# A depthwise causal convolution moved from TensorE (diagonal matmuls) to VectorE (multiply-adds with a per-partition scalar)

## The reference

```
mixed = einsum('btd,cd->btc', x, W_qkv)                  # 3072 channels
c = conv_general_dilated(mixed^T, conv_w, padding=[(K - 1, 0)],
                         feature_group_count=CONV_DIM)   # K = 4 taps, one filter per channel
mixed = silu(c); q, k, v = split(mixed)                  # 16 heads of 64
beta = sigmoid(x W_b); g = -exp(A_log) * softplus(x W_a + dt_bias)
S = S * exp(g_t) + k_t (v_t b_t)^T;   o_t = q_t S        # scan over time
out = out * rsqrt(mean(out^2) + 1e-6) * silu(z)
x = x + out W_out
W = einsum('abcd,cefg->abefdg', G1, G2)                  # FFN weights, real and imaginary
x = x + complex_linear(layernorm(x), W_real, W_imag)
```

## Time and profile before

| what | us |
|---|---|
| runs of the kernel before | 2817.29 and 2794.29, median 2805.79 |
| profiled execution, its own time | 2800.42 |
| its span on the slowest core (core 4) | 2798.9 |
| spans of the eight cores | 2769.6 to 2798.9 |

### The profile page before, as it was taken

The page is one execution under the profiler, slowest core; times in us unless marked ns, Lnnn a source line. Parts: engine busy times, 40 slices in busy tenths (PEclk is TensorE's granted clock), DMA queues, the critical chain, the costliest instruction groups (busy, mean ns, idle before and its releaser), DMA issues.

```text
span 2798.9 us, 17445 instructions; the slowest of 8 cores (2769.6 to 2798.9 us)
## 1 busy us (share of the span) xinstructions
PE 1217.3 (43%) x5440; PEld 478.7 (17%) x5440; DVE 707.4 (25%) x1023; ACT 342.2 (12%) x570; POOL 124.6 (4%) x217
## 2 busy tenths in 40 slices
PE   0005427246254276244447434437624444743444
PEld 0002112021121131021122011213101112201121
DVE  1143141240331410222330222232022223022322
ACT  0001102002011011011102111111201110211111
POOL 1230000000000000100000000000010000000000
PEclk9999557556575585556567556668556666755666
DMA  8654210201101201200011110010220001011001
GB/s 127 144 168 84 40 19 17 26 19 42 1 20 42 19 4 45 6 19 20 19 42 23 27 5 19 19 42 19 49 6 19 19 19 42 20 29 6 19 19 27
DMA packets 149624, 94.79 MB, mean 34 GB/s; under 512 B 133291, under 2 KB 134064, under 8 KB 149536
## 3 DMA queue, kind: packets, MB, share of 16 engines
q0 software_dynamic: 43360, 36.00, 10.8%
q1 hardware_dynamic: 106176, 57.69, 7.3%
HBM read 99.76 MB, written 11.67 MB: 40 GB/s over the span
## 4 chain that ended last, share of the span: by engine, by line
PE 42%; DVE 19%; DMA 15%; ACT 10%; issue 8%; DVEq 2%; POOL 2%; ACTq 1%; POOLq 0%; SPq 0%
PE ps L281 35%; DMA s_gamb<-scr 4%; ACT s_mixed L281 4%; PE psS L281 4%; PE psT L281 3%; DVE s_dsb L281 3%; DMA s_eaq<-scr 3%; DVE s_bn L281 3%; DMA s_dsb<-convdiag 3%; DVE s_Sall L281 2%; ACT L281 2%; DVEq L280 2%; ACT s_dsb L281 2%; DVE s_x2a L281 1%; DVE s_gatedc L281 1%
## 5 line engine op out<-in xcount | busy, mean ns | idle before, releaser
L281 PE MATMUL ps<-s_mixed,s_dwin 128*128 128x512 bf16 x640 | 296.9, 617 | 178.1 <-ACT s_mixed L281 143.6
L281 PE MATMUL ps<-s_lnxT,s_wqkvT 128*128 128x512 bf16 (+1 forms) x1344 | 299.7, 387 | 9.2 <-DVE s_lnxT L281 7.9
L281 PE MATMUL psT<-s_i128b,s_lnx 128*128 128x128 bf16 x256 | 32.4, 307 | 393.7 <-DVE s_lnx L281 393.7
L281 PEld LDWEIGHTS ps<-s_lnxT,s_wqkvT 128*128 128x128 bf16 x1344 | 132.8, 101 | 174.5 <-issue 35.8
L281 PE MATMUL psT<-s_i128b,s_mixed 128*128 128x128 bf16 x512 | 58.8, 286 | 206.4 <-DMA s_a<-s_dsb 84.6
L281 PE MATMUL psT<-s_i128b,s_gatedc 128*128 128x128 bf16 x256 | 32.4, 307 | 248.7 <-DVE s_Sbf L281 161.2
L281 PEld LDWEIGHTS ps<-s_mixed,s_dwin 128*128 128x128 bf16 x640 | 69.0, 126 | 402.5 <-issue 402.0
L281 ACT ACTIVATE s_mixed<-ps 128x512 bf16<-128x512 f32 x160 | 95.8, 599 | 326.9 <-PE ps L281 326.9
L281 DVE COPY s_mixed<-s_halo 128x72 bf16<-128x72 bf16 x8 | 1.8, 227 | 464.8 <-ACT s_mixed L281 464.8
L281 DVE CAST s_mixed<-ps 128x512 bf16<-128x512 f32 (+1 forms) x88 | 57.9, 658 | 238.5 <-PE ps L281 238.5
L281 PE MATMUL ps<-s_wbig,s_gatedT 128*128 128x512 bf16 x256 | 96.9, 562 | 15.8 <-DVE s_gatedT L281 15.8
(11 more groups left out here) (119 smaller groups left out, 1174.7 us busy)
## 6 DMA issues: line engine op xcount, KB each, us to landing
s_dwin<-diagbf SPq DMA_DIRECT2D x160, 128.0 KB, 2.2
s_xa<-xpre SPq DMA_DIRECT2D x16, 512.0 KB, 4.3
s_xa<-xown SPq DMA_DIRECT2D x16, 512.0 KB, 3.9
s_xr<-xown SPq DMA_DIRECT2D x16, 512.0 KB, 4.0
s_wqkvT<-wqkvT POOLq DMA_DIRECT2D x1, 6144.0 KB, 41.9
s_eaq<-scr POOLq DMA_DIRECT2D x32, 128.0 KB, 5.4
y<-s_x2a SPq DMA_DIRECT2D x8, 512.0 KB, 2.9
y<-s_x2b SPq DMA_DIRECT2D x8, 512.0 KB, 2.9
```

What stands on the lines that cost most here:

```text
L281: r = a(*args, **kw)
```

## The change

The diagonal matrices go, with their six rounds of load and store, the scratch, the 160 loads of `dwin`, and the 640 matmuls. In their place the host packs the taps into `convw`, 128 x 96 f32 (one column for each chunk and tap), which SP loads once. VectorE computes each chunk in f32 in one of two halves of `z_chunk` (512 columns each, free at this point): one tensor_scalar for the first tap, then three scalar_tensor_tensor (multiply by the tap, add the sum so far). ScalarE's Silu reads that half and writes the chunk in `mixed`, as before. From the third chunk on VectorE waits for the Silu of two chunks earlier. The wait of VectorE for the six stores before the first tile goes; a wait for SP's small loads comes in behind the memsets.

```
-    d_diagbf = nc.dram_tensor("diagbf", [24, 4, 128, 128], BF16, kind="Internal").ap()
...
+    sL.inc(SY.dma_start(out=convw_sb[:], in_=d_convw), 16)
...
     sV.inc(V_.memset(ones16f[:], 1.0))
-    for grp in range(6):
-        p0 = grp * 16
-        if grp > 0:
-            s_dgm.wait(G_)
-        s_dg.inc(G_.dma_start(
-            out=dsb_t[:].rearrange("p (f c) -> p f c", f=16),
-            in_=diag_flat[p0:p0 + 16].rearrange("f p c -> p f c")), 16)
-        s_dg.wait(SY)
-        s_dgm.inc(SY.dma_start(
-            out=diagbf_flat[p0:p0 + 16].rearrange("f p c -> p f c"),
-            in_=dsb_t[:].rearrange("p (f c) -> p f c", f=16)), 16)
+    sL.wait(V_)
...
-    s_dgm.wait(V_)
...
+        accs = [z_chunk[:, 0:512], z_chunk[:, 512:1024]]
+        sS.wait(V_)
+        conv_vf = {}
+        conv_sf = {}
         for i_cc, cc in enumerate(cc_list):
-            dhalf = i_cc % 2
+            acc = accs[i_cc % 2]
+            base = cc * 515
             if i_cc >= 2:
-                w = evac_cnt.get(("conv", i_cc - 2))
-                SY.wait_ge(w[0].h, w[1])
-            s_dw[dhalf].inc(SY.dma_start(
-                out=dwin[:, dhalf * 512:(dhalf + 1) * 512].rearrange("p (f c) -> p f c", f=4),
-                in_=diagbf_flat[cc * 4:(cc + 1) * 4].rearrange("f p c -> p f c")), 16)
-            s_dw[dhalf].wait(T)
-            sV.wait(T)
-            sS.wait(T)
-            ph = ps2[:, dhalf * 512:(dhalf + 1) * 512]
-            for tapn in range(4):
-                sT.inc(T.matmul(ph, dwin[:, dhalf * 512 + tapn * 128: dhalf * 512 + (tapn + 1) * 128],
-                                mixed[:, cc * 515 + tapn: cc * 515 + tapn + 512],
-                                start=(tapn == 0), stop=(tapn == 3)))
-            evac_cnt[("conv", i_cc)] = (sT, sT.fence())
-            sT.wait(S_)
-            sS.inc(S_.activation(out=mixed[:, cc * 515 + 3: cc * 515 + 515], in_=ph,
+                sS.wait(V_, conv_sf[i_cc - 2])
+            V_.tensor_scalar(out=acc, in0=mixed[:, base: base + 512],
+                             scalar1=convw_sb[:, cc * 4: cc * 4 + 1],
+                             scalar2=None, op0=ALU.mult)
+            for tapn in (1, 2, 3):
+                V_.scalar_tensor_tensor(
+                    out=acc, in0=mixed[:, base + tapn: base + tapn + 512],
+                    scalar=convw_sb[:, cc * 4 + tapn: cc * 4 + tapn + 1],
+                    op0=ALU.mult, in1=acc, op1=ALU.add)
+            conv_vf[i_cc] = sV.fence()
+            sV.wait(S_, conv_vf[i_cc])
+            sS.inc(S_.activation(out=mixed[:, base + 3: base + 515], in_=acc,
                                  func=AF.Silu))
+            conv_sf[i_cc] = sS.fence()
         sS.wait(V_)
```

More of the change, by code:

```diff
@@ L57, in host_prep @@
     bi = np.asarray(inputs["L0_ffn_bias_imag"], np.float32)
-    convdiag = np.zeros((24, 4, 128, 128), np.float32)
-    idx = np.arange(128)
+    convw = np.zeros((128, 96), np.float32)
     for cc in range(24):
         for tap in range(4):
-            convdiag[cc, tap, idx, idx] = conv_w[cc * 128 + idx, 0, tap]
+            convw[:, cc * 4 + tap] = conv_w[cc * 128: (cc + 1) * 128, 0, tap]
     mneg = np.where(np.arange(128)[:, None] > np.arange(128)[None, :],
@@ L85, in host_prep @@
             [W_a, np.zeros((16, 1024), np.float32), W_b], 0).T),
-        convdiag=convdiag,
+        convw=convw,
         i128=np.eye(128, dtype=np.float32),
@@ L132, in build_program @@
     d_wabT = nc.dram_tensor("wabT", [D, 48], F32, kind="ExternalInput").ap()
-    d_diag = nc.dram_tensor("convdiag", [24, 4, 128, 128], F32, kind="ExternalInput").ap()
+    d_convw = nc.dram_tensor("convw", [128, 96], F32, kind="ExternalInput").ap()
     d_i128 = nc.dram_tensor("i128", [128, 128], F32, kind="ExternalInput").ap()
@@ L175, in build_program @@
     wbig = sb("s_wbig", [128, 8 * D])
-    dwin = sb("s_dwin", [128, 2 * 512])
+    convw_sb = sb("s_convw", [128, 96], F32)
     i128b = sb("s_i128b", [128, 128])
@@ L335, in build_program @@
     sV.inc(V_.memset(ones16f[:], 1.0))
-    diag_flat = d_diag.rearrange("cc tap p c -> (cc tap) p c")
-    diagbf_flat = d_diagbf.rearrange("cc tap p c -> (cc tap) p c")
-    for grp in range(6):
-        p0 = grp * 16
-        if grp > 0:
-            s_dgm.wait(G_)
-        s_dg.inc(G_.dma_start(
-            out=dsb_t[:].rearrange("p (f c) -> p f c", f=16),
-            in_=diag_flat[p0:p0 + 16].rearrange("f p c -> p f c")), 16)
-        s_dg.wait(SY)
-        s_dgm.inc(SY.dma_start(
-            out=diagbf_flat[p0:p0 + 16].rearrange("f p c -> p f c"),
-            in_=dsb_t[:].rearrange("p (f c) -> p f c", f=16)), 16)
+    sL.wait(V_)
     ffnbuf = [(z_chunk[:, 0:512], z_chunk[:, 512:1024]),
```

## The result

The changed kernel takes 2858.24 us (median of 11 runs, 2837.0 to 2880.73), the kernel before beside it 2817.13 us (10 runs, 2792.04 to 2834.48). The ratio is 1.0168, interval 1.0122 to 1.0214. The forecast was 2798 us and no change that can be measured; the time lies above its range, 2757 to 2848. The profiled execution took 2856.23 us, with a span of 2854.7 us on the slowest core, core 5.

A forecast was written before the change was run, and what follows sets the result against it. Two stretches with one chain alone on the path: the setup's six load-store rounds, and the convolution's matmul-Silu turns in eight tiles. Setup -46 and convolution +44 from 2800.4 us gave 2798 us, range 2757 to 2848.

The forecast's parts named there:

- Setup: Setup: removing the six rounds gains 45.4 us, FFN load 3.7 more, activation loads cost 3; sum 46, between 43 and 49.
- The 3 us taken for the activation loads beside the weights: Setup: activation loads move to the span's start and share the weights' time, at most 6.2 us late; the middle, 3, taken.
- the first FFN product: Setup, sign to look for: VectorE's first FFN product near 68 us instead of 113.6.
- Convolution: Convolution stage: 160 chunks at 3.05 us plus 8 x 2.65 on VectorE, 509 us against 464.8 idle before: 44 us lost.
- The price of the per-partition scalar: Convolution on VectorE: a per-partition scalar adds 60 ns to each operation, giving 752 ns for an STT, 487 for the tensor_scalar.
- Rivals 1, 2 and 3: Convolution on VectorE: scalar free, 2760 us (0.10); tensor_scalar at one element a cycle, 2840 (0.15); STTs at half rate, 3054 (0.03).
- rival 4: Setup gives less: activation loads cost all 6.2 us and FFN loads keep 3.7; 39 gained against 44 lost, 2805 us; chance 0.12.
- The clock: Convolution stage and square sums: granted clock stays at 0.50, 1.2 GHz, so taking the matmuls away cannot slow what follows.
- Sum. -46 + 44 = -2 us.: Whole kernel: setup gain and convolution loss nearly cancel, from 2800.4 us to 2798 us; chance 0.60.
- What can move is the 48 groups of 16 wide matmuls: Four last tiles: a group takes 6.50 or 4.93 us by clock level; a quarter moved is 19 us, either side.
- The base: Whole kernel: the profiled execution of the kernel before, 2800.4 us (span 2798.9), from which the forecast was counted.

The follow-up runs named there:

- the hold: Odd core of each pair held some 21 us by two memsets before the tile loop: changed kernel 2792.62 us (0.9918), kernel before 2795.85 us (0.9929).
- the small hold: Kernel before, with its odd cores held some 5 us by one memset of 2860 columns before the tile loop: 2867.63 us, ratio 1.0124.

## Why the prediction was wrong, point by point

- **Setup, "46 us, between 43 and 49".** Right: 45.6. The 3 us taken for the activation loads beside the weights measured 3.24, and by just these the first FFN product came at 71.50 and not near 68.
- **Convolution, "One chunk ... 3.05 us", 44 us lost.** Right: 3.06 us and 46.3. The price of the per-partition scalar, read from two other operations, held within a nanosecond (752 forecast, 751 measured), and the one-source tensor_scalar from bf16 to f32 runs as fast as the cast the other way with that price on top (487). Rivals 1, 2 and 3 are out, and with 45.6 us from the setup so is rival 4. The Trainium skill's Vector Engine (DVE) Microarchitecture Reference, section 7, warns that an STT with two non-bf16 sources in SBUF halves its throughput. The new STT has one bf16 source, so the warning does not cover it, and 480 of them took 751 ns for 512 columns. The row that it does cover, two f32 sources at 336.20 in the earlier trace rows, took 0.68 us for 512 columns, so this case's trace does not agree with the warning.
- **The clock.** Right: 0.50 to 0.51 in the stage and in the square sums behind it.
- **"Sum. -46 + 44 = -2 us."** Right as a sum of what the change does: with the hold the two kernels differ by 0.1%, with `s_gamb` off DRAM by 0.2%, neither of which is clear of the noise.
- **The step that failed: "What can move is the 48 groups of 16 wide matmuls", 19 us either side.** I let a shift in time act on one thing only, TensorE's clock, and so put the change of every wait behind the convolution at nothing. The wide matmuls hardly moved: 414.8 us of a core's time, against 411.4 before (means of the cores). What moved were the waits for the small loads, which I had left out of the sum because their code is untouched: on the slowest core from 161.2 to 196.3 us for `s_gamb` and from 43.3 to 63.6 for `s_eaq`, 55.4 us together. They depend on when the neighbouring core issues the same loads, and that is a matter of a few us of timing, which every edit to the setup changes. The row with the wait stood in the profile of before, the largest wait for a transfer behind the setup, and its eight times ran from 13.06 to 18.05 us for one and the same load. That spread needed an explanation before a sum could be made.
- **The base.** The execution I counted from had its pairs 3 to 5 us apart at the first tile and drifting away from each other. It took 2800.42 us; the median of ten runs is 2817.13. Most of the scatter that I read as noise is the same effect: with the hold the ten runs of the kernel before lie within 7.8 us (2790.47 to 2798.24), without it ten lie within 42.4.

What stays open is the last link, why the shorter setup leaves the pairs closer. At the first norm the cores of a pair stand 4.7 us apart in the mean in the kernel before (profiled execution), 5.3 and 5.2 in the two kernels that got the rounds back, 4.9 in the kernel before with `s_gamb` by a matmul, and 2.5 to 3.4 in the changed kernel and the other kernels without rounds and hold. Pair by pair it is 3.7 to 6.3 us in the 16 pairs of the four kernels with rounds, and 0.7 to 5.4 in the 20 pairs of the five without. So the rounds spread the pairs; how they do it was not tried. Nor does a good start settle the rest: with the rounds back, one pair that issued its loads 6.1 us apart at the first tile had drifted to 1.9 by the last, and lost 80 us. That kernel stays 1.2% above the 1.016 that the sum gives it, though its pairs start as far apart as those of before. What makes pairs drift from tile to tile was not tried either.

## What to carry to other kernels

A wait for a small transfer that varies from tile to tile in the profile of before, for the same bytes, is an unpriced term: before a sum of a few us is trusted, find what it varies with, and look at the neighbouring core at the same time. Where all cores run one program, a change that only shifts time can cost or gain more than the work it moves; two kernels are compared fairly when the shared cause is taken out of both, here by holding every second core. And a few numbers that have to reach all partitions are spread faster by a mask and a small matmul (1.4 us) than by two loads of 16-byte pieces (10.8 us in the mean far from the neighbour's, 20.4 in step).

## What the runs showed of the hardware

- Two cores of a pair slow each other's loads of small pieces from DRAM although next to nothing is moved. Two loads of 8 KB, each in 512 pieces of 16 bytes, land 10.8 us after the issue of the second where the pair is 13 us and more apart, and after 20.4 us under 2 us apart. In both cases the DMA engines count as busy (0.81 of ten such us with the hold, 0.84 of twenty in step) at 1 to 2 GB/s. The traces record each load as 16 packets of 512 bytes: under 2 us apart the longest packet took 9.04 us in 44 of 56 cases, beyond 13 us 4.52 us in 128 of 198, half as long. That looks as if something served the two cores in turn; what it is, no run shows. The Trainium skill's HBM Reference, Specifications (TRN2), says that the two cores of a domain share its bandwidth and that a change bound by DMA should be timed with the pair active. The runs agree that the pair is what counts, but at 1 to 2 GB/s it is hardly bandwidth that runs short here.
- In step is a state that can hold itself: where both cores wait equally long, they leave the wait as close as they came. Cores 4 and 5 of the changed kernel stayed 1.6 to 1.7 us apart for four tiles, and cores 2 and 3 of the kernel before with the small hold were under 4 us apart at all eight `s_gamb` loads.
- The per-partition scalar costs VectorE some 60 ns an instruction, as in the earlier trace rows, also where instructions follow each other without a wait for another engine: 751 ns for the STT of 128x512, against 692 for the f32 product of the same size.
